# The last two attention groups turned into freed PSUM banks, and two out projections moved behind the last weighing but one

## The reference

```python
q, k, v = split(layer_norm(x) @ qkv_w + qkv_b)        # 12 heads of 16, windows of 14 x 14
attn = softmax(q @ k.T * scale + rel_h + rel_w)       # relative position bias from q
x = x + (attn @ v) @ proj_w + proj_b                  # the out projection
x = x + gelu(layer_norm(x) @ fc1_w + fc1_b) @ fc2_w + fc2_b
```

## Time and profile before

| | |
|---|---|
| median of 3 runs | 326.77 us (326.68 to 326.79) |
| the profiled execution | 324.05 us |
| its span, first to last instruction | 322.2 us |
| PE busy | 307.8 us, 96% of the span |
| DVE, ACT, POOL busy | 183.8, 136.6, 90.0 us |
| TensorE's granted clock | full in all 40 slices |
| chain that ended last | PE 80%, DVE 10%, SP's queue 3%, DMA, issue and POOL 2% each |

### The profile page before, as it was taken

The page is one execution under the profiler, slowest core; times in us unless marked ns, Lnnn a source line. Parts: engine busy times, 40 slices in busy tenths (PEclk is TensorE's granted clock), DMA queues, the critical chain, the costliest instruction groups (busy, mean ns, idle before and its releaser), DMA issues.

```text
span 322.2 us, 9218 instructions
## 1 busy us (share of the span) xinstructions
PE 307.8 (96%) x3886; PEld 232.2 (72%) x3886; DVE 183.8 (57%) x423; ACT 136.6 (42%) x296; POOL 90.0 (28%) x205
## 2 busy tenths in 40 slices
PE   6999999999988999999999999999999899999996
PEld 3457688898765459978846768888877446997476
DVE  5745776877859101236873676687876810354572
ACT  3575145554564450023257414655556454012420
POOL 4000874424620087000000086542661004000000
PEclk9999999999999999999999999999999999999999
DMA  7982000000030011100031100000000000000003
GB/s 210 392 304 60 13 9 17 14 3 5 3 132 27 0 50 72 51 24 2 0 101 31 30 3 11 15 12 7 3 5 1 2 0 0 2 0 1 2 2 99
DMA packets 10236, 13.81 MB, mean 43 GB/s; under 512 B 3473, under 2 KB 8305, under 8 KB 10194
## 3 DMA queue, kind: packets, MB, share of 16 engines
q1 hardware_dynamic: 9570, 13.12, 12.9%
q10 hardware_dynamic: 624, 0.09, 0.2%
HBM read 10.95 MB, written 0.79 MB: 36 GB/s over the span
## 4 chain that ended last, share of the span: by engine, by line
PE 80%; DVE 10%; SPq 3%; DMA 2%; issue 2%; POOL 2%; ACT 1%; DVEq 0%
PE banks L1203 10%; PE banks L1078 10%; PE banks L1221 10%; PE banks L1108 10%; PE banks L1034 7%; PE banks L997 5%; PE banks L1128 5%; PE banks L968 3%; PE banks L1387 3%; PE banks L957 2%; PE banks L1234 2%; SPq L771 2%; PE banks L1281 2%; PE banks L1010 2%; PE banks L1251 1%
## 5 line engine op out<-in xcount | busy, mean ns | idle before, releaser
L1477 ACT ACTIVATE arena<-banks 128x392 f32<-128x392 f32 (+1 forms) x112 | 49.1, 491 | 46.5 <-PE banks L1108 46.5
L1666 DVE TENSOR_REDUCE negmax<-banks 128x4 f32<-128x784 f32 (+1 forms) x48 | 46.1, 961 | 18.2 <-PE banks L1078 17.7
L1078 PE MATMUL banks<-attention_arena 32*128 32x196 f32 x384 | 48.8, 353 | 0.9 <-DVE negmax L1661 0.4
L1108 PE MATMUL banks<-attention_arena 32*128 32x196 f32 x384 | 46.4, 336 | 2.0 <-DMA attention_arena<-negmaxT 1.5
L1108 PE MATMUL banks<-attention_arena,keys 32*128 32x196 f32 x384 | 45.1, 326 | 0.0
L1078 PE MATMUL banks<-keys,attention_arena 32*128 32x196 f32 x384 | 44.0, 323 | 0.0
L1108 PEld LDWEIGHTS banks<-attention_arena 32*128 32x128 f32 x384 | 30.7, 184 | 6.8 <-issue 3.4
L1203 PE MATMUL banks<-yT,fc 128*128 128x512 f32 (+1 forms) x96 | 33.3, 607 | 0.0
L1221 PEld LDWEIGHTS banks<-fc,arena 128*128 128x128 f32 x192 | 31.1, 190 | 1.5 <-ACT arena L1498 1.5
L1108 PEld LDWEIGHTS banks<-attention_arena,keys 32*128 32x128 f32 x384 | 32.0, 184 | 0.0
L1221 PE MATMUL banks<-fc,arena 128*128 128x192 f32 x192 | 31.7, 327 | 0.0
(11 more groups left out here) (192 smaller groups left out, 551.9 us busy)
## 6 DMA issues: line engine op xcount, KB each, us to landing
fc<-in_fc SPq DMA_DIRECT2D x2, 768.0 KB, 4.9
fc<-in_fc SPq DMA_DIRECT2D x2, 576.0 KB, 5.2
attention_arena<-negmaxT SPq DMA_DIRECT2D x68, 1.0 KB
rel<-in_rel SPq DMA_DIRECT2D x2, 448.0 KB, 5.1
x_tok<-in_x SPq DMA_DIRECT2D x4, 192.0 KB, 4.1
inverse<-in_inverse SPq DMA_DIRECT2D x1, 768.0 KB
inverse<-in_space_back SPq DMA_DIRECT2D x1, 768.0 KB, 4.3
qkv<-in_qkv SPq DMA_DIRECT2D x1, 576.0 KB, 4.0
```

What stands on the lines that cost most here:

```text
L1078: ins = mm(o, asking, asked, start=not with_rel, stop=bool(with_rel))
L1108: last = mm(m.bank[4 + j][key_rows(b), cols * tile:cols * (tile + 1)], keys_of(n, j, tile)[with_rel], queries_of(n, j, tile)[with_rel], st ...
L1477: run(m.probsT[keys, n % P_RING, j, 0:cols], m.bank[4 + j][keys, 0:cols], ACT.Exp).then_inc(s.probs, 1)
L1666: dve.tensor_reduce(at[rows, 2 * tiles * part:2 * tiles * (part + 1)].rearrange("k (j a) -> k j a", a=tiles), m.banks[rows, 2 * part:2 * p ...
```

## The change

- `turned_in(n, j)` is new: groups 0 to 11 are turned into banks 4 to 7 as before, group 12 into banks 0 to 3, group 13 into banks 0, 5, 6, 7.
- Weigh 10 and 11 go to bank 4, weigh 12 to bank 2, weigh 13 to bank 3. Out 0 to 3 go to banks 1, 4, 6, 7.
- Weigh 10 stands after the first half of turn 11's pair 1 instead of behind all of it, and ACT copies it before the exps of pair 1 instead of behind them. ACT copies weigh 11 behind all four exps of group 12 instead of behind two.
- Turn 12 waits for the last maximum (`s.max` 28) and no longer for all exps of group 11. Turn 13 waits for the first exp of group 12 instead of for all four.
- Out 0 stood between weigh 11 and turn 13, out 1 between weigh 12 and weigh 13. Both now stand between weigh 12 and weigh 13.
- On DVE the add and the statistics of image 0 stood between invert 11 and invert 12; they now stand behind invert 12, before those of image 1.
- A wait of out 3 for the copy of weigh 13 falls away, since they no longer share bank 7.

```diff
 def out_bank(b):
-    return b if b < 2 else 4 + b
+    return (1, 4, 6, 7)[b]
+
+def turned_in(n, j):
+    if n < N_GROUPS - 2:
+        return 4 + j
+    return (j, (0, 5, 6, 7)[j])[n - (N_GROUPS - 2)]
 def weighed_in(n):
-    return {N_GROUPS - 4: 0, N_GROUPS - 3: 2, N_GROUPS - 2: 3, N_GROUPS - 1: 7}.get(n, 4 + n % 2 if n < 2 * IMAGES else 4)
+    return {N_GROUPS - 2: 2, N_GROUPS - 1: 3}.get(n, 4 + n % 2 if n < 2 * IMAGES else 4)
...
                     if n == 0:
                         pe.wait_ge(s.bias_scaled, 2)
+                    elif n == N_GROUPS - 2:
+                        pe.wait_ge(s.max, 2 * N_GROUPS)
+                    elif n == N_GROUPS - 1:
+                        pe.wait_ge(s.probs, 4 * (n - 1) + 1)
                     elif pair == 0:
                         pe.wait_ge(s.probs, 4 * n - 2)
                     else:
                         pe.wait_ge(s.probs, 4 * n)
...
-                if weighed_in(n) in (4, 5):
+                if n < N_GROUPS - 3:
                     pe.wait_ge(s.probs, 4 * (BATCHES[batch_of(n)][-1] + 1) + weighed_in(n) - 3)
                 else:
                     pe.wait_ge(s.probs, 4 * (n + 1))
-                    pe.wait_ge(s.max, 2 * N_GROUPS - 1 if weighed_in(n) == 0 else 2 * N_GROUPS)
+                    pe.wait_ge(s.pv_out, N_GROUPS - 3)
...
-                            if q == (3 if last_scored(n) else 1):
+                            if q == 1:
                                 for weighed in WEIGHED_AT.get(n, ()):
                                     weigh(l, weighed)
...
-                    for b in range(2):
-                        if n == OUT_AT[b] + 1:
-                            if b == 0:
-                                pe.wait_ge(s.pv_out, N_GROUPS - 3)
-                            out_project(s, wl, b)
+                out_project(s, wl, 0)
+                out_project(s, wl, 1)
                 weigh(l, N_GROUPS - 1)
                 out_project(s, wl, 2)
                 turn_norm(s.ln[1], 4, 0)
-                pe.wait_ge(s.pv_out, N_GROUPS)
                 out_project(s, wl, IMAGES - 1)
...
-                        if pair == last_scored(n):
+                        if pair == (n == N_GROUPS - 2):
                             for weighed in WEIGHED_AT.get(n, ()):
                                 take_weighed(weighed)
...
-                    if n > OUT_AT[0]:
-                        add_output(n - OUT_AT[0] - 1)
-                        take_stats(s.ln[1], n - OUT_AT[0] - 1)
+                for b in range(2):
+                    add_output(b)
+                    take_stats(s.ln[1], b)
```

More of the change, by code:

```diff
@@ L367, in place_in_batch @@
     return slice(at, at + MAIN_KEYS)
-def last_scored(n):
-    return n + AHEAD + 1 == N_GROUPS
 def sums_turned(i):
@@ L1098, in turn @@
                         pe.wait_ge(s.probs, 4 * n)
-                    if n >= 3 and (n % 2 == 1 or n >= 2 * IMAGES + 2):
-                        pe.wait_ge(s.pv_out, n - 2 if len(BATCHES[batch_of(n - 2)]) == 2 else min(n - 1, N_GROUPS - 4))
+                    if 3 <= n < N_GROUPS - 2 and (n % 2 == 1 or n >= 2 * IMAGES + 2):
+                        pe.wait_ge(s.pv_out, n - 2 if len(BATCHES[batch_of(n - 2)]) == 2 else n - 1)
                     at, landed = max_landed(n)
@@ L1107, in turn @@
                             pe.wait_ge(s.pv_out, n - 1)
-                        last = mm(m.bank[4 + j][key_rows(b), cols * tile:cols * (tile + 1)], keys_of(n, j, tile)[with_rel],
+                        last = mm(m.bank[turned_in(n, j)][key_rows(b), cols * tile:cols * (tile + 1)], keys_of(n, j, tile)[with_rel],
                                   queries_of(n, j, tile)[with_rel], start=not with_rel, stop=bool(with_rel))
@@ L1476, in attention @@
                         for j in (2 * pair, 2 * pair + 1):
-                            run(m.probsT[keys, n % P_RING, j, 0:cols], m.bank[4 + j][keys, 0:cols], ACT.Exp).then_inc(s.probs, 1)
+                            run(m.probsT[keys, n % P_RING, j, 0:cols], m.bank[turned_in(n, j)][keys, 0:cols], ACT.Exp).then_inc(s.probs, 1)
                         if pair == 0 and n == 3:
```

## The result

| | before | after |
|---|---|---|
| runs | 326.79, 326.68, 326.77, 325.80 us | 323.23, 322.01, 322.14, 323.30 us |
| median | 326.73 us | 322.69 us |
| ratio | | 0.9882, 95% interval 0.9851 to 0.9914 |
| profiled execution, its span | 324.05, 322.2 us | 323.23, 321.3 us |

The changed kernel is faster by 1.2%, 4.04 us; forecast were 1.88 us and a range of 324.3 to 325.6. The two profiled executions are only 0.8 us apart. The runs of before stand close together or 1 us lower, those of after in two pairs 1.2 us apart. Three executions further down were disturbed (330.58 us for the profiled one of no_rows_wait, 1732.94 and 1065.65 us for two of before) and are left out. So the first question is how much of the 4.04 us is the change, and the second how much of it the tails account for.

The account below looks back on a forecast made before the run. PE was taken as the bound (80% of the chain), with 1.25 us of waits in each of two tails; 0.94 us gained per tail, 1.88 us in all, took 326.77 to 324.9 us, range 324.3 to 325.6.

Parts of the forecast that it names:

- the last of the sum: Whole kernel: the runs' median stays 2.72 us above the profiled execution, so 326.77 less 1.88 gives 324.9 us.
- The mis-sized term: PE's tail: out 0 and out 1 back to back keep their lengths of 1.47 and 1.50 us.
- Splitting turn 11: PE's tail: putting weigh 10 into the middle of turn 11's pair 1 costs 0.10 us.
- Turn 12's wait for exps: PE's tail: the wait of 0.25 us for exp 11 ahead of turn 12 goes; turn 12 starts at 86.51.
- The row DMAs: Turn 13 waits for group 13's maxima, 1.14 us behind SP's last issue's end, and starts at 89.06.
- The forecast that the profile would name the DMA: Sign at turn 13, about 89.06: the profile gives "DMA attention_arena<-negmaxT" as what ended the wait.
- The price of 0.21: Turn 13: waiting for its row DMAs from 88.85 to 89.06 gives back 0.21 us of the gain.
- DVE's thin cover: DVE behind invert 12: image 0's add and statistics end at 94.30, 0.18 us ahead of image 1's add.
- Rival 2: DVE becomes the bound if invert 12 is late: 0.2 to 0.4 us a layer lost, 325.3 to 325.7 us; 8%.
- Rivals 3 and 4: No change, POOL or ACT holding the tail: 326.2 to 327.4 us, 5%; slower, turn 13 beyond 90.00: 4%.
- The estimate by the Trainium skill's figure: Turn 13's row DMAs at 2.0 us each: start at 89.37, gain 0.63 us a layer, 325.5 us; within an 8% rival.

Follow-up runs that it names:

- no_rows_wait: Changed kernel, but turn 13 reads image 2's queries and bias rows and group 13's row wait stands behind weigh 12: lowest level 321.3 us against 321.86.
- control_after: The changed kernel run again, unchanged: levels at 321.86, 323.54 and 324.65 us (9 runs), ratio to before 0.992.
- move_only: Kernel before with only out 0 and out 1 behind weigh 12 and their adds behind invert 12, old banks: 325.03, 326.59, 327.90 us by level, ratio 1.003.
- banks_only: Changed kernel with out 0 back between weigh 11 and turn 13 and the adds back in place: 324.04, 325.78, 327.02 us by level, ratio 0.9996.
- warm_4: Changed kernel with four warm-up products instead of three: 321.80 to 322.50 us in 6 runs, median 321.93.
- before_warm_4: Kernel before with four warm-up products instead of three: 324.09 to 324.62 us in 12 runs, median 324.30, ratio to before 0.9945.
- control_before: The kernel before run again, unchanged: levels at 324.14, 325.59 and 326.87 us (12 runs), ratio to before 0.9993.

## Why the prediction was wrong in its number

**The step that failed** is the last of the sum: "The median of the runs is 2.72 above the profiled one; I take the difference over". The profiled execution at 324.05 us was of the lowest level, the three runs shown of the upper one. Those 2.72 us are no constant around the span but the distance of the two levels (2.76 by the table): TensorE at about half speed between 6.7 and 14 us, which an execution of either kernel may have or not. The four runs of after had 0 or 1.2 us of it, and that was chance: at equal level the forecast was near, 322.17 against 321.86 for the lowest, and 324.9 against 324.65 (two runs) for the upper.

**The tails** went as the steps said, up to one term. On the common clock, forecast and control_after: weigh 10 at 84.94 and 84.95; weigh 11 at 88.05 and 87.95; turn 13 at 89.06 and 89.07; weigh 12 at 90.60 and 90.61; out 0 at 91.40 and 91.41; weigh 13 at 94.37 and 94.20; the transposes at 97.75 and 97.58. The mis-sized term is out 0 and out 1: 1.47 + 1.50 = 2.97, measured 2.79. I put the difference down to the change-over to a step of another kind, which either length held and of which there is one less back to back; no run tests that. In move_only, with the old banks, the two back to back take 2.80 (95.94 to 98.74), so it goes with the order and not with the banks. The gain of a tail is 1.11 instead of 0.94 us. The trace thus has 2.2 us, the levels 2.2 to 2.4; for the last 0.1 or 0.2 I have no row.

**Splitting turn 11** was priced at 0.10 and cost nothing: from 84.16 to weigh 11 at 87.95 is 3.79 us, the sum of 1.45, 0.80 and 1.54 without waits. The term had no effect, since turn 13 then waited for its rows.

**Turn 12's wait for exps** is gone, as said, and by itself worth nothing (banks_only).

**The row DMAs.** The start of turn 13 by the lag of 1.14 us was right to 0.01. The forecast that the profile would name the DMA was not: it names ACT, and only the experiments decide it. The price of 0.21 was low: it is 0.31 (1.12 less 0.81), for PE was free at 88.75.

**DVE's thin cover** held. The add of image 0 ran from 93.01 and its statistics ended at 94.22, that of image 1 came at 94.31, 0.11 behind weigh 13's start as before. The cover was 0.09 us and not 0.18, since out 1 ended earlier than forecast. Rival 2 did not occur. ACT was better placed than I had it: six exps in one row from 86.76 to 89.45, and the copy of weigh 11 at 89.41 instead of 89.96. Rivals 3 and 4 named places that the trace shows without a wait (out 1, weigh 13) or at the predicted time (turn 13). The estimate by the Trainium skill's figure of 2.0 us for a DMA (DMA: Bandwidth & Descriptors, Anatomy of one DMA, the table of the fixed cost) had turn 13 at 89.37; measured is 89.07. The page gives that figure for DMAs issued by GpSimd; these are issued by SP, small and from SBUF to SBUF, and for them the row was the better guide.

## What to carry to other kernels

To cover a wait that another engine sets, look for work that may run in its place, and give that work its own banks: here the reordering without the banks cost 0.8 us, the banks without the reordering gave nothing, and both gave 2.3. Before a profiled time is brought to a median of runs, look at whether all are of one level; three runs within 0.1 us of one another can all be of the upper one. When a bracket names an engine for a start that your sum puts down to a DMA, move the DMA and see.

## What the runs showed of the hardware

- TensorE's start decides up to 2.8 us of a 324 us kernel, and differs between executions of the same kernel on the same chip: 10, 8 and 14 of 32 runs of before at 324.2, 325.8 and 327.0 us. With three warm-up products and 0.9 to 1.4 us of idle behind them, the stretch from the transposes to 14 us ran at 2.4 GHz, partly at 1.2 (granted clock 0.50 from 8.6 to 11.6 us in the profile of the changed kernel), or, by the lengths of its rows, at half speed throughout (eight transposes 1.94 us instead of 1.07). With a fourth product and no idle, all 18 runs of warm_4 and before_warm_4 were of the lowest level. The Trainium skill (TensorE: Matmul & The Clock Gate, What's actually happening) describes a clock gate that gives 1.2 GHz by default and 2.4 after activity, and whose watch on the activity runs freely and doesn't start with the kernel. That the same program falls into different levels agrees with that; no run here shows the phase itself.
- A start that waited for four DMAs of 0.5 to 1 KB came 1.15 us behind the last issue's end (87.92 to 89.07), as it had with the other group (1.14).
- Two out projections back to back took 2.79 us (control_after) and 2.80 us (move_only); apart they took 1.47 and 1.50, together 2.97.
- A profile can lack the granted clock, and a mean of 1.0 is then no proof of full speed: control_before's view prints 1.00 where eight transposes took 1.94 us instead of 1.07.
